# Attention scores from bf16 parts on 72 rows, and one more head of four summed by TensorE

## What is computed

```python
q = (h @ Wq.T + bq) * 8**-0.5; k = h @ Wk.T + bk       # per sequence: 256 x 128
p_h = softmax(q_h @ k_h.T)                              # 16 heads of 8 features
mix = softmax((16 * exp(-|i-j|/16) + sum_h p_h) / 16)   # 256 x 256
n1 = LN1(h + mix @ h);  n2 = LN2(n1)
h  = LN3(n2 + W2 @ relu(W1 @ n2 + b1) + b2)             # hidden size 512
# before the first layer h = layernorm(x); after the last x = x + h
```

## Time and profile before

| | |
|---|---|
| median of 3 executions | 2278.96 us (2277.47 to 2282.62) |
| profiled execution | 2278.32 us, span from first to last instruction 2276.4 us |
| attention stage | from about 8 to 1265 us of the span |
| busy share in 500 to 1200 us | PE 95%, DVE 90%, ACT 83%, POOL 68% |
| granted clock of PE there | 1.00 |

### The profile page before, as it was taken

How to read it: one execution, slowest core, us unless ns; L and a number is a source line. 1 busy time by engine, 2 the same in 40 slices (tenths; PEclk the granted TensorE clock), 3 DMA queues, 4 the chain that set the end, 5 groups by cost and what they waited for, 6 DMA issues and landing times. The chain is left out here.

```text
span 2276.4 us, 40732 instructions
## 1 busy us (share of the span) xinstructions
PE 1981.4 (87%) x9638; PEld 1254.6 (55%) x9638; DVE 1714.8 (75%) x4069; ACT 1647.2 (72%) x5239; POOL 1263.4 (56%) x2137
## 2 busy tenths in 40 slices
PE   4899999999999999999997784949995888898886
PEld 2455555555555555555555463336652666666665
DVE  5999999899899989999995425068876666766673
ACT  3888888788888878888884231459962778787874
POOL 2566766676667667667666333048874434443440
PEclk9999999999999999999998797869996999999999
DMA  1000000000000000000000311102212000000000
GB/s 44 1 1 4 7 13 4 3 17 4 5 7 13 4 3 17 4 4 7 13 1 1 130 53 48 30 19 93 101 56 72 1 1 1 1 1 1 1 1 19
DMA packets 30509, 45.93 MB, mean 20 GB/s; under 512 B 9352, under 2 KB 21904, under 8 KB 29952
## 3 DMA queue, kind: packets, MB, share of 16 engines
q1 hardware_dynamic: 29008, 40.52, 5.6%
q0 software_dynamic: 1248, 2.59, 0.3%
HBM read 39.34 MB, written 5.32 MB: 20 GB/s over the span
## 5 line engine op out<-in xcount | busy, mean ns | idle before, releaser
L405 ACT ACTIVATE a_prob<-a_scores,a_negmax 128x256 f32<-128x256 f32 x1536 | 706.2, 479 | 122.0 <-DVE a_negmax L506 91.7
L506 DVE TENSOR_REDUCE a_negmax<-a_scores 128x2 f32<-128x512 f32 x768 | 525.5, 685 | 53.3 <-PE a_scores L628 44.8
L628 PE MATMUL a_scores<-a_km,a_qT 32*128 32x512 f32 x1536 | 436.3, 646 | 63.2 <-ACT a_prob L405 56.2
L639 PE MATMUL a_heads<-a_prob,a_diag 128*128 128x256 f32 x1536 | 391.3, 388 | 11.0 <-POOL a_diag L308 7.5
L308 POOL TENSOR_TENSOR a_diag<-ident,a_rowinv 128x256 f32<-128x256 f32 x384 | 240.9, 632 | 157.4 <-DVE a_rowinv L547 150.3
L405 ACT ACTIVATION_READ_ACCUMULATOR a_prob<-a_scores,a_negmax 128x1 f32 x1536 | 323.2, 210 | 0.0
L639 PEld LDWEIGHTS a_heads<-a_prob,a_diag 128*128 128x128 f32 x1536 | 280.5, 193 | 62.8 <-POOL a_diag L308 25.1
L628 PEld LDWEIGHTS a_scores<-a_km,a_qT 32*128 32x128 f32 x1536 | 117.3, 184 | 196.2 <-issue 98.3
L1374 DVE TENSOR_TENSOR_SCAN c_state<-c_decay,c_psD 128x1024 f32<-128x1024 f32 x64 | 146.1, 2286 | 34.2 <-PE c_psD L1477 23.3
L1238 POOL TENSOR_TENSOR c_du<-c_state,c_c_row 128x1024 f32<-128x1024 f32 x64 | 151.3, 2366 | 33.6 <-DVE c_state L1374 24.3
L486 DVE SCALAR_TENSOR_TENSOR a_sums<-a_prob,a_rowinv,a_sums 128x256 f32<-128x256 f32 x288 | 141.1, 490 | 29.0 <-DVE a_rowinv L547 2.0
(11 more groups left out here) (286 smaller groups left out, 4282.8 us busy)
## 6 DMA issues: line engine op xcount, KB each, us to landing
c_c_row<-c_rows SPq DMA_DIRECT2D x32, 512.0 KB, 3.6
a_w<-in_a_w SPq DMA_DIRECT2D x12, 256.0 KB, 2.6
b_w<-in_b_w SPq DMA_DIRECT2D x1, 2816.0 KB, 15.2
a_rows<-in_a_rows SPq DMA_DIRECT2D x12, 128.0 KB, 2.0
b_w<-in_b_w SPq DMA_DIRECT2D x1, 1536.0 KB, 18.2
d_wqkv<-in_d_wqkv SPq DMA_DIRECT2D x2, 768.0 KB, 5.7
b_rows_in<-in_b_blank SPq DMA_DIRECT2D x1, 1518.0 KB, 8.8
b_packed<-b_rows_in SPq DMA_DIRECT2D x5, 264.0 KB, 4.2
```

What stands on the lines that cost most here:

```text
L405: ins = a.activation(prob[part % RING][:, c, :], psS[part % 2][:, c, :], ACT.Exp, bias=negmax[part % 2][:, c:c + 1], accum_out=rowsum[part ...
L506: v.tensor_reduce(negmax[part % 2][:, hs], psS[part % 2][:, hs, :], AX.X, ALU.max, negate=True).then_inc(s["negmax_ready"], 1)
L628: p.matmul(psS[part % 2][:, h * BH:(h + 1) * BH, :], qT[u][rows, t * P:(t + 1) * P], km[u][rows, c:c + BH, :], start=True, stop=True)\
L639: ins = p.matmul(psH[:, t, :], diag[part % RING][:, h, :], prob[part % RING][:, h * BH + 1, :], start=(j == 0 and h == 0), stop=(j == HG - ...
```

## The change

**Scores.** ACT writes q and k into one float32 tile `qk`, and then a bfloat16 copy of both as the first of three parts. POOL subtracts it (`rest`), copies the rest to bfloat16 as the second part, and subtracts that to get the third (`split`, three instructions of 128x512). SP writes the parts to a scratch tensor in DRAM (128 x 6 runs of 512 bytes) and, when that has landed, reads them back twice, into a tile of keys and one of queries with 72 rows (3 x 3 pairs of parts x 8 features) and all 16 heads beside each other (`spread`, one transfer of 576 KB and three of 192 KB). PE then makes one bfloat16 product of 72 rows x 256 columns for each head, which adds all nine products of parts. The rows of the weight matrices are permuted on the host so that a head's features lie apart.

**Order.** `project` moves from 6 slots ahead of the scores to 10, `split` stands at 9 and `spread` at 8 ahead. In a round that is slot 6 for `project`, 7 for `split` and 0 for `spread`, instead of slot 2 and 3 for `project` and `mask`. SP no longer has a loop of its own: its loads stand in the same table, behind the spreads.

**Sums.** In the second group of heads of each row tile (`ALONE`), PE sums three heads and DVE one: `sum_b` is left out there, and `diag` is 384 columns wide.

```diff
+ALONE = (1,)
+ADDS = QSLOTS - TPS * len(ALONE)
+PARTS = 3
+KROWS = PARTS * PARTS * DH
+SPREAD = 16 + PARTS * 16 + 16
...
-                place(at - 8, "per_layer", l, q, 0)
-            place(at - 6, "project", l, q, 0)
-            place(at - 5, "mask", l, q, 0)
+                place(at - 12, "per_layer", l, q, 0)
+            place(at - 10, "project", l, q, 0)
+            place(at - 9, "split", l, q, 0)
+            place(at - 8, "spread", l, q, 0)
...
+            if q == SEQS - 1 and l + 1 < LAYERS:
+                for part, slot in enumerate((-7, 25, 30, 34, 40)):
+                    place(at + slot, "load", l, q, part)
...
+def summed(j):
+
+    return range(1, CH) if j in ALONE else range(1, CH, BH)
...
+                    if kind == "spread":
+                        sp.wait_ge(s["split_step"], (m + 1) * 4)
+
+                        sp.wait_ge(s["spread_in"], m * SPREAD + SPREAD)
+                        sp.dma_start(scratch.rearrange("k a p t -> p (k a) t"),
+                                     parts3[:].rearrange("p k a t -> p (k a) t")).then_inc(s["spread_in"], 16)
+                        sp.wait_ge(s["spread_in"], m * SPREAD + 16 + SPREAD)
+
+                        sp.wait_ge(s["scores_ready"], ((m - 2) * G8 + G8 + 2 * G8) * HALVES)
+                        sp.dma_start(spread[u][1][:], keys).then_inc(s["spread_in"], 16)
+                        for a in range(PARTS):
+                            sp.dma_start(spread[u][0][a * PARTS * DH:(a + 1) * PARTS * DH], queries(a))\
+                                .then_inc(s["spread_in"], 16)
...
-                    elif kind == "mask":
-                        g.wait_ge(s["qk_ready"], m * 2 + 2)
-
-                        g.wait_ge(s["scores_ready"], ((m - 2) * G8 + G8 + 2 * G8) * HALVES)
-                        g.tensor_tensor(km[u][:], kT[:].unsqueeze(1).broadcast_to([P, CH, L]),
-                                        head_mask[:].unsqueeze(2).broadcast_to([P, CH, L]), ALU.mult)\
-                            .then_inc(s["km_ready"], 1)
+                    elif kind == "split":
+                        g.wait_ge(s["split_step"], m * 4 + 1)
+                        g.tensor_tensor(rest[:], qk[:], parts3[:, :, 0], ALU.subtract).then_inc(s["split_step"], 1)
+                        g.wait_ge(s["split_step"], m * 4 + 2)
+                        g.tensor_tensor(parts3[:, :, 1], rest[:], one[:].unsqueeze(2).broadcast_to([P, 2, L]), ALU.mult).then_inc(s["split_step"], 1)
+                        g.wait_ge(s["split_step"], m * 4 + 3)
+                        g.tensor_tensor(parts3[:, :, 2], rest[:], parts3[:, :, 1], ALU.subtract)\
+                            .then_inc(s["split_step"], 1)
...
-                run(g, do, first=("diag",), last=("mask",))
+                run(g, do, first=("diag",), last=("split",))
...
+                        a.wait_ge(s["spread_in"], (m - 1) * SPREAD + 16 + SPREAD)
+                        a.activation(parts3[:, :, 0], qk[:], ACT.Copy).then_inc(s["split_step"], 1)
...
-                    elif kind == "sum_b":
+                    elif kind == "sum_b" and part % HG not in ALONE:
                         sum_b(m, u, part)
...
-                        for h in range(HALVES):
-                            rg = (j % 2) * HALVES + h
-                            rows = slice(rg * RW, (rg + 1) * RW)
-                            c = j // 2 * BH
-                            p.matmul(psS[part % 2][:, h * BH:(h + 1) * BH, :], qT[u][rows, t * P:(t + 1) * P],
-                                     km[u][rows, c:c + BH, :], start=True, stop=True)\
-                                .then_inc(s["scores_ready"], 1)
+                        for c in range(CH):
+                            ins = p.matmul(psS[part % 2][:, c, :], spread[u][0][:, j * CH + c, t * P:(t + 1) * P],
+                                           spread[u][1][:, j * CH + c, :], start=True, stop=True)
+                            if c % BH == BH - 1:
+                                ins.then_inc(s["scores_ready"], 1)
...
-                        for h in range(HALVES):
-                            ins = p.matmul(psH[:, t, :], diag[part % RING][:, h, :], prob[part % RING][:, h * BH + 1, :],
-                                           start=(j == 0 and h == 0), stop=(j == HG - 1 and h == HALVES - 1))
+                        for k, c in enumerate(summed(j)):
+                            ins = p.matmul(psH[:, t, :], diag[part % RING][:, k, :], prob[part % RING][:, c, :],
+                                           start=(j == 0 and k == 0), stop=(j == HG - 1 and c == CH - 1))
```

More of the change, by code:

```diff
@@ L159, in stage_a, with queries @@
         hT = sb("hT", [P, NTOK])
[L160 to L164 removed]
+        qk = sb("qk", [P, 2, L])
+        rest = sb("rest", [P, 2, L])
+        one = sb("one", [P, 2])
+        parts3 = ctx.enter_context(nc.sbuf_tensor("a_parts3", [P, 2, PARTS, L], BF16))
+        spread = [[ctx.enter_context(nc.sbuf_tensor(f"a_spread{u}_{k}", [KROWS, HEADS, L], BF16)) for k in range(2)]
+                  for u in range(2)]
+        scratch = nc.dram_tensor("a_split", (2, PARTS, P, L), BF16, kind="Internal").ap()
+        keys = scratch[1].rearrange("a (e h) t -> (a e) (h t)", h=HEADS).unsqueeze(0)\
+            .broadcast_to([PARTS, PARTS * DH, HEADS * L])
+        def queries(a):
+            return scratch[0, a].rearrange("(e h) t -> e (h t)", h=HEADS).unsqueeze(0)\
+                .broadcast_to([PARTS, DH, HEADS * L])
         RING = QSLOTS
@@ L169, in stage_a @@
         negmax = two("negmax", [P, CH])
-        diag = [sb(f"diag{u}", [P, BH, P]) for u in range(RING)]
+        diag = [sb(f"diag{u}", [P, CH - 1 if u % HG in ALONE else BH, P]) for u in range(RING)]
         acc = two("acc", [P, TPS, L])
@@ L274, in _ @@
+                run(sp, do)
             @block.gpsimd
```

97 lines of the change are left out of this document (48 added, 49 removed).

## The result

The change makes the kernel slower. The median is 2617.5 us (2614.4 to 2620.8, 4 runs) against 2278.2 us (2277.3 to 2282.6, 4 runs) of the kernel before on the same chip: ratio 1.1485, 95% interval 1.1464 to 1.1506. The forecast was 2475 us with a range of 2385 to 2555. Direction and the main mechanism were right, the size was not: +339 us, of which 142 were not forecast, and the time lies 62 us over the range.

A forecast was written before the change was run, and what follows sets the result against it. A closed loop over POOL, DVE and the ACT path was taken to bound the round, 24.5 us growing to 28.4. 2278.3 + 168 (rounds) + 20 (norm rows) + 12 - 4 (start) = 2474, say 2475 us; range 2385 to 2555.

The forecast's parts named there:

- The loop of three legs: Attention round: POOL from norm 3's statistics 6.34 us, DVE applying norm 1 0.81, slots 2 to 7 17.36; together 24.51.
- Leg 1: In the table, POOL from norm 3's rstd to norm 1's gain, 8.01 us before; the prediction's shorter leg 1 was 6.34.
- the rest: Table column, not a forecast term: from norm 1's gain on POOL to norm 3's next rstd, 16.57 us before.
- Split: Three POOL instructions in slot 7, ahead of norm 1's rstd: adds 3.65 us to leg 1, ends 2.85 and 3.97.
- 43 x 3.9 = +168: Full attention rounds: each grows from 24.5 to 28.4 us, +3.9, in 43 rounds, +168 us.
- the likeliest case: Whole kernel: the forecast with its own unknowns in split, bank and norm rows, 2420 to 2515 us, chance 0.55.
- Bank order: PE in the third leg: mlp must wait for ACT's copy of the turned mix, 0.25 us a round, ends 0 and 0.5.
- Scores and head sums at no cost: PE: bfloat16 scores, 0.7 us a block, and one more head sum in slots 0 and 4 lie beside the path; cost 0.
- Rival A, the clock: PE's clock halves after waits for diag: +1.0 us a round, up to 2.5; 2518 us, up to 2580; chance 0.25.
- Spread, on SP: DRAM write and reads between split and next scores: 4 + 6 us, hidden by over 6 slots, cost 0 a round.
- The next layer's norm rows: Five layer boundaries: SP's loads come later, POOL waits 5.5 to 8.5 us; 4 us each, 20 in all, ends 0 and 40.
- Start: Stage start: copy, split, write and reads before the first scores, +12 us; first rounds without norms gain, -4.

The follow-up runs named there:

- split in slot 0 with wide reads and loads ahead: Changed kernel with the split one slot later, behind norm 1's rstd, plus wide reads and loads ahead: 2483.7 us.
- wide reads: Changed kernel with the threefold repetition of the spread's reads moved behind the rows, outer length 24 and 8 instead of 3: 2489.1 us alone.
- loads ahead: Changed kernel with the next layer's small loads placed ahead of a spread in SP's order instead of behind it: 2474.2 us alone.
- early order: Project, split and spread moved four slots earlier (slots 2, 3, 4), against the changed kernel with wide reads and loads ahead: 2281.6 us, ratio to before 0.9990.
- narrow reads: Early order and loads ahead, but with the changed kernel's own reads of outer length 3: 2288.3 us; with ALONE empty as well, 2292.2 us.

## Why the prediction was right in direction and wrong in size

- **The loop of three legs** was right. Leg 1 of the table grew by 3.37 us, the rest by 0.49 (medians instead of means: 3.49 and 0.39), and a longer split goes in one to one.
- **Split**, 3.65 us in the sum, measured 3.47: inside 2.85 to 3.97. The groups by shape after (mean ns) are 1154 for a subtraction to float32, 1039 for the copy and 1167 for a subtraction to bfloat16; the row of 1268 was too high for them, and the lower estimate of 3.3 + 0.16 us that the prediction set beside its sum was nearer.

```profile
L344 POOL TENSOR_TENSOR a_parts<-a_rest,a_parts 128x512 bf16<-128x512 f32 x48 | 56.0, 1167 | 3.8
L340 POOL TENSOR_TENSOR a_rest<-a_qk,a_parts 128x512 f32<-128x512 f32 x48 | 55.4, 1154 | 9.5 <-ACT a_parts L441 9.5
L342 POOL TENSOR_TENSOR a_parts<-a_rest,a_one 128x512 bf16<-128x512 f32 x48 | 49.9, 1039 | 3.8
```

- **43 x 3.9 = +168** for the full rounds: measured 154 to 164 by the account above. (The unknowns of the likeliest case, added up straight, give 2410 to 2520 and not 2420 to 2515; the range covers both.)
- **Bank order**, +0.25: PE does wait for the copy of the turned mix, 0.63 us in the round shown, and the rest of the round grew by 0.5 us in all. Right in kind; no experiment separates it.

```profile
720.02 2.05 PE L716 MATMUL a_turn<-a_w,a_act 128*128 128x128 f32 x16 [0.63 <-ACT a_mixT L471]
```

- **Scores and head sums at no cost**: right for the third head sum, which a run took away; for the scores it rests on PE's waits. The page after has them at 310 ns and 443 ns each, with PE idle 243.3 us before head sums for a `diag`:

```profile
L682 PE MATMUL a_heads<-a_prob,a_diag 128*128 128x256 f32 x1728 | 518.6, 443 | 244.1 <-POOL a_diag L352 243.3
...
L670 PE MATMUL a_scores<-a_spread,a_spread 72*128 72x256 bf16 x1536 | 276.0, 310 | 173.5 <-ACT a_prob L450 127.2
```

- **Rival A, the clock** (+1.0 to 2.5 us a round): the clock does fall. In a round where PE waits long for the `diag`, the next four products take twice their time:

```profile
730.92 2.08 PE L682 MATMUL a_heads<-a_prob,a_diag 128*128 128x256 f32 x4 [3.22 <-POOL a_diag L352]
```

  That is 2.08 instead of 1.03, 1.2 GHz instead of 2.4, and the granted clock of 731 to 736 is 0.50. But the rest of the round grew by 0.5 us in all, the bank order included: some 20 us over 43 rounds, and not the 1.0 to 2.5 us a round of the rival. That is a net figure, as two of DVE's sums left the same stretch, so the clock's own part isn't shown. In the other kernels of the table with the split between norm 2's bias and norm 1's gain, the rest is 0.5 to 1.3 us over before; what it comes from isn't shown either. No kernel was run that keeps PE busy in the wait.
- **The failed step** is "Spread, on SP ... 1024 KB lands in 5.1 us, so I take 4 + 6 us with issue", and with it "The next layer's norm rows ... I take 4 us for each, 20 in all; ends 0 and 40". The transfer of the earlier trace rows moves some 200 GB/s; the reads move 75 and take 16 us and not 6. In a plain round that stays hidden, as the prediction had it; at a boundary it doesn't. So the norm rows wait 18 us and not 5.5 to 8.5, and two kinds of load that I hadn't considered (the projection's columns and the second MLP's weights) wait too, as SP's order puts each behind a spread. Together 149 us instead of 20; removing either the slowness or the order gave 128 and 143 us back.
- **Start**, +12 - 4: measured +11.6 over the first four intervals. The first scores come at 54.37 instead of 31.18, 23 us later, of which a part is won back by the fourth interval. The near agreement is luck: from their issue the reads alone took 18 us and not 6.

## What to carry over

A step that is hidden "since it has six slots" is still paid for by whatever stands behind it in its queue: for a large transfer, list the small urgent ones issued after it, and put them ahead. Take a transfer's time from one with the same outer length, not only the same bytes. And for a chain that is closed over several engines, an added instruction is free only outside the stretch in which its engine works without a pause; here a shift by four slots with the transfers put right was worth 336 us, and the cheaper TensorE work next to nothing (2281.6 us against 2283.5 of the kernel before, on the same chip).

## What the hardware showed that I hadn't expected

- Three read transfers of 192 KB and one of 576 KB ran on 0.19 of the DMA engines, at 75 GB/s; with another order of the same dimensions 0.69 and 209 GB/s in a stretch of 2 us. A load issued behind the slow ones had 104 of its 128 packets started within 0.9 us; the other 24 started 12 us later.
- VectorE's float32 TENSOR_SCALAR of 128x128 slows down beside GpSimd's operations: one that starts while GpSimd works on 256 columns or more ends 0.08 us after that operation does, in 290 of the 295 such cases in four traces (before, after, split in slot 0 with wide reads and loads ahead, early order). Alone it takes 0.33 us, beside the `diag` of 0.61 us it takes 0.63 (before, 25 of norm 1's 54 between 500 and 1160 us), and wholly beside a split instruction of 1.16 us 1.18 (after). Normalizing norm 3 takes 347 ns on average before, and 748 after, where part of it runs beside the split's end:

```profile
L528 DVE TENSOR_SCALAR a_n<-a_h,a_f,a_mv 128x128 f32<-128x128 f32 x54 | 16.4, 347 | 0.0
```

```profile
L573 DVE TENSOR_SCALAR a_n<-a_h,a_f,a_mv 128x128 f32<-128x128 f32 x42 | 29.7, 748 | 0.0
```

  Row maxima beside the same split keep their 0.68 us. The Trainium skill ("VectorE: DVE Perf Modes", section "Two Vector instructions with no wait between them") says in its definitions that an operation in a two-port mode reads through an interface shared with GpSimd; that fits, but the trace doesn't name the mode.
- The rounds at the loop's jump are longer when the spreads run (30.0 to 31.0 us with wide reads, 28.7 to 28.8 with narrow ones, 27.4 to 27.7 before; with narrow reads the next round is 25.1 to 25.6 instead of 24.2 to 24.3, so the two together differ little). With wide reads in the early order DVE then stands for 5.9 to 6.9 us with nothing to wait for that the profile shows, before the first instruction of the new pass:

```profile
631.66 0.18 DVE L593 RECIPROCAL a_rowinv<-a_rowsum 128x4 f32<-128x4 f32 x1 [5.93 <-issue]
```

  Before, it is 2.7 to 3.0 us at the same place, and with narrow reads 2.8 to 3.2. The trace also lists packets of the kind "instruction": around the jump they stand at most 2.0 us apart before, and up to 3.8 to 5.3 us in the early order with wide reads (none between 623.62 and 628.91). That the two go together is seen; that one causes the other no run shows.
